# Transposed attention scores: the mask product is replaced by a tile that GpSimd writes, one slot later

## The reference

```python
q = proj(query, w_q, b_q); k = proj(key, w_k, b_k); v = proj(value, w_v, b_v)
scores = jnp.einsum('bhqd,bhkd->bhqk', q, k) / np.sqrt(D_K)
scores = jnp.where(mask, scores, -jnp.inf)      # mask: j <= i
attn = jax.nn.softmax(scores, axis=-1)
out = jnp.einsum('bhqk,bhkd->bhqd', attn, v)
...
x = x + jnp.tanh(g_xattn[0]) * _L0_xattn_ref(_layernorm(x, axis=-1), ctx_1024, ctx_1024, ...)
x = x + jnp.tanh(g_ffn[0]) * _L0_ffn_ref(_layernorm(x, axis=-1), ...)
```

## Time and profile before

| | us |
|---|---|
| median of 3 runs | 938.75 (936.92 to 939.47) |
| the profiled execution | 942.84 |
| its span | 940.9 |

### The profile page before, as it was taken

One profiled execution on the slowest core, in us unless ns is written; L12 is line 12 of the kernel. 1 busy time (PEld: TensorE's weight loads), 2 busy tenths in 40 slices (PEclk: granted clock), 3 DMA queues, 4 the chain that ended last, 5 costly groups with the idle time before them and its releaser, 6 DMA issues. The chain is left out here.

```text
span 940.9 us, 24425 instructions
## 1 busy us (share of the span) xinstructions
PE 846.5 (90%) x7600; PEld 750.5 (80%) x7601; DVE 600.4 (64%) x1521; ACT 442.3 (47%) x962; POOL 257.6 (27%) x239
## 2 busy tenths in 40 slices
PE   3599999999999999999539999999999999999990
PEld 2488888888888888888338789998989998989980
DVE  2357888888888888887636555555555555555540
ACT  2155555655555555654224444554444455544440
POOL 3001333222332333323210322232332232223332
PEclk9699999999999999999659999999999999999996
DMA  8765666665667787864388432323233233322222
GB/s 185 141 135 132 158 152 129 139 155 156 155 159 202 188 185 176 174 164 156 130 288 295 87 53 48 54 53 53 48 50 52 48 59 50 51 48 36 30 24 25
DMA packets 87944, 108.77 MB, mean 116 GB/s; under 512 B 12832, under 2 KB 81568, under 8 KB 85664
## 3 DMA queue, kind: packets, MB, share of 16 engines
q1 hardware_dynamic: 72448, 87.17, 37.4%
q0 software_dynamic: 14304, 19.15, 12.7%
q10 hardware_dynamic: 1088, 1.11, 0.4%
HBM read 46.82 MB, written 34.36 MB: 86 GB/s over the span
## 5 line engine op out<-in xcount | busy, mean ns | idle before, releaser
L1220 POOL DMA_INDIRECT out_rows<-yg,xs x78 | 126.6, 1624 | 332.7 <-ACT yg L1262 190.3
L1352 PE MATMUL bank<-xh,wts 128*128 128x256 f16 x1872 | 214.2, 275 | 0.0
L1368 PE MATMUL bank<-wts,hh 128*128 x1872 | 210.6, 273 | 0.0
L1352 PEld LDWEIGHTS bank<-xh,wts 128*128 x1872 | 185.0, 99 | 22.5
L1368 PEld LDWEIGHTS bank<-wts,hh 128*128 128x128 f16 x1872 | 183.2, 98 | 21.2
L1252 ACT ACTIVATE hf<-bank,b1t,gscale 128x256 f32<-128x256 f32 x312 | 154.7, 562 | 24.3 <-PE bank L1352 24.3
L979 PE MATMUL bank<-va,probs 128*128 128x102 f32 x1024 | 139.7, 278 | 8.1 <-DVE ao L696 8.1
L979 PEld LDWEIGHTS bank<-va,probs 128*128 128x128 f32 x1024 | 124.2, 192 | 10.7 <-DVE ao L696 6.2
L1262 ACT ACTIVATE yg<-yb,xs 128x256 f32<-128x256 f32 x78 | 35.4, 500 | 199.5 <-DVE yb L1301 199.5
L583 ACT ACTIVATE probs<-bank 128x512 f32<-128x512 f32 x128 | 76.9, 601 | 101.8 <-PE bank L962 95.2
L1291 DVE SCALAR_TENSOR_TENSOR hh<-hf,hscale,hh 128x512 f16<-128x512 f32 x156 | 117.1, 751 | 5.6
(11 more groups left out here) (169 smaller groups left out, 1082.0 us busy)
## 6 DMA issues: line engine op xcount, KB each, us to landing
wts<-in_W SPq DMA_DIRECT2D x16, 1024.0 KB, 7.9
wts<-keys SPq DMA_DIRECT2D x96, 128.0 KB
wts<-queries SPq DMA_DIRECT2D x96, 128.0 KB
xs<-token_rows SPq DMA_DIRECT2D x39, 272.0 KB
split_weights<-wts SPq DMA_DIRECT2D x8, 1024.0 KB, 4.6
wts<-split_weights SPq DMA_DIRECT2D x8, 1024.0 KB
xin<-in_x SPq DMA_DIRECT2D x16, 256.0 KB, 4.0
cin<-in_ctx_in SPq DMA_DIRECT2D x16, 256.0 KB, 4.2
```

What stands on the lines that cost most here:

```text
L1220: pool.indirect_dma_start(out=out[:, :], out_offset=bass.IndirectOffsetOnAxis(ap=numbers, axis=0), in_=yg[m % 2][:, half, :], in_offset=No ...
L1352: last = pe.matmul(HB[c // 2][:, c % 2 * TILE:(c % 2 + 1) * TILE], wts[:, bass.ds(expert[1], 1), at:at + P], xh[b][:, xp, k, :], start=q = ...
L1368: last = pe.matmul(YB[b][:, half * D:(half + 1) * D], hh[b][:, hp, c, half * P:(half + 1) * P], wts[:, bass.ds(expert[0], 1), at:at + D], ...
```

## The change

GpSimd now makes one tile `cover` per quad, 128 queries by 4 x 128 keys. Where the key is not after the query it holds the query's row maximum, elsewhere 1e30. It does this with one `affine_select`, from `rowmax` broadcast along the keys. Four products of this tile with the negative identity then bring both the maxima and the mask into the transposed scores, and the product of identity and mask is gone. The transposed scores of a quad run two slots behind its scores, not one, and the exponentials with them; the probabilities' products stay three slots behind. The row maxima's buffer is now freed by the select (`cover_ready`), the cover's by the transposed scores. `cover` lies in memory of the expert stage's first input tiles, which the attention stage doesn't use. GpSimd's indirect DMAs go from slots 4, 5, 6, 7 to 3, 4, 6, 7.

```diff
-MASKED = -1e30
+MASKED = 1e30
...
+        cover = [env["first_xs"][0][:, :, :].rearrange("p h r -> p (h r)")[:, 256 * i:256 * i + 256].bitcast(BF16)
+                 .rearrange("p (a k) -> p a k", a=4) for i in range(2)]
...
                 def it(g, par, half, stays, stayed):
                     for n in range(QUADS):
+                        if there(g):
+
+                            pool.wait_ge(max_ready, g * QUADS + n + 1)
+                            settled(pool)
+                            when(pool, n >= 2 or there(g - 1), st_psum, g * QUADS + n - 1)
+                            settled(pool)
+                            pool.affine_select(out=cover[n % 2][:, :, :],
+                                               in_=rowmax[n % 2][:, :].unsqueeze(2).to_broadcast([P, 4, P]),
+                                               compare_op=ALU.is_ge, fill=MASKED, base=0, pattern=[[0, 4], [-1, P]],
+                                               channel_multiplier=1).then_inc(cover_ready, 1)
                         if n in (1, 5) and there(g - 1):
                             b = n // 4
                             pool.wait_ge(var2_ready, (g - 1) * GT + b + 1)
...
-                        if n >= 4 and there(g - 2):
-                            b, r = (n - 4) // 2, n % 2
-                            if n == 4:
+                        if n in (3, 4, 6, 7) and there(g - 2):
+                            b, r = divmod((3, 4, 6, 7).index(n), 2)
+                            if n == 3:
...
-                        q, pg = (QUADS - 1, g - 1) if n == 0 else (n - 1, g)
+                        q, pg = (QUADS + n - 2, g - 1) if n < 2 else (n - 2, g)
...
-                            when(dve, n >= 2 or there(g - 1), st_psum, g * QUADS + n - 1)
+                            when(dve, n >= 2 or there(g - 1), cover_ready, g * QUADS + n - 1)
...
-                        if there(g if n >= 1 else g - 1):
-
-                            tg, m, i = (g, n - 1, par) if n >= 1 else (g - 1, QUADS - 1, p1)
+                        if there(g if n >= 2 else g - 1):
+
+                            tg, m, i = (g, n - 2, par) if n >= 2 else (g - 1, QUADS + n - 2, p1)
                             tok = slice((m // 4) * P, (m // 4) * P + P)
-                            pe.wait_ge(max_ready, tg * QUADS + m + 1)
+                            pe.wait_ge(cover_ready, tg * QUADS + m + 1)
                             when(pe, m >= 2 or there(tg - 1), exp_ready, tg * QUADS + m - 1)
                             ps = TB[m % 2]
-                            pe.matmul(ps[:, :], ident16[:, :], maskT[:, :].unsqueeze(1).to_broadcast([P, 4, P]),
-                                      start=True, stop=False)
-                            for a in range(4):
-                                pe.matmul(ps[:, a * P:(a + 1) * P], rowmax[m % 2][:, a:a + 1].to_broadcast([P, P]),
-                                          negident[:, :], start=False, stop=False)
                             for a in range(4):
                                 h = 4 * (m % 4) + a
+                                pe.matmul(ps[:, a * P:(a + 1) * P], cover[m % 2][:, a, :],
+                                          negident[:, :], start=True, stop=False)
                                 last = pe.matmul(ps[:, a * P:(a + 1) * P], kst[i][:, h, tok],
-                                                 qst[i][:, h, tok], start=False, stop=a == 3)
+                                                 qst[i][:, h, tok], start=False, stop=True)
```

## The result

| | median us (lowest to highest) |
|---|---|
| before | 939.04 (936.92 to 939.47) |
| after | 1022.34 (1020.48 to 1023.27) |

The ratio is 1.0889, with an interval from 1.0866 to 1.0913: the change costs 8.9%. The forecast was 961 with a range of 935 to 984. The direction was right, the size was not: +83 us in place of +22.

The account below looks back on a forecast made before the run. TensorE was taken to bound each group up to slot 4's residual, a VectorE chain from there to `ao`. Per group -0.86 + 1.56 + 0.3 = +1.0, together +14, clock +8: +22, so 961 us, range 935 to 984.

Parts of the forecast that it names:

- the queue and the chain: Slots 4 to 7: the power waits behind slot 5's select, `norm2` starts 1.56 us later, VectorE's work grows 5.88 to 7.44.
- the clock term: Attention groups: TensorE's pauses of 2.0 and 1.6 us lower its clock in half the groups or more, costing 8 us.
- it falls in every group: Rival, attention groups: the clock falls in every group, nearly all exposed, 25 us instead of 8, giving 978; chance 0.15.
- the first part: Slot 0 to slot 4's second output projection: TensorE drops five masks, 1.08 us, but VectorE's lateness leaves 0.86 saved.
- contention: Shared port: the select after row maximum 2 meets a two-input VectorE instruction, costing 0.3 us per group (0 to 0.9).
- so the lateness stays: Behind slot 1's select: `norm2` is 0.53 us later; VectorE, busy 7.32 of 7.79 us up to 310.46, stays late.
- the end of the stage: End of the attention stage: one slot more in the drain costs about 0.5 us.
- the 953 of the prediction: Sign of a wrong forecast: a granted clock of 1.00 throughout would put the result near 953.
- The port rival: Selects 0, 2, 3, 6, 7 block two-input VectorE instructions, up to 0.9 us each; 15 us more, 976; chance 0.15.
- `norm2` beside `xb`: Slot 5: `norm2` takes 1.36 us beside `xb`, cited as agreeing with two-input VectorE and GpSimd instructions excluding each other.
- The faster rival: Attention groups: the two-slot lag lifts TensorE's waits and powers are not held; 36 us gained, about 901; chance 0.12.
- a mask product taken from TensorE inside them gives nothing: From slot 4's residual to `ao`, 5.88 us: VectorE sets the pace, so dropping mask products there gains nothing.

Follow-up runs that it names:

- filled: The changed kernel plus unread products in TensorE's two pauses, 16 in slot 6 and 12 in slot 7: 969.4 us, ratio 1.0327.
- both powers first: The changed kernel with GpSimd's power for `rs2` moved ahead of the select in slots 1 and 5: 960.7 us, ratio 1.0231.
- both powers first and the pauses filled: The changed kernel with the powers ahead of the selects and 16 unread products in slot 7 alone: 936.2 us, ratio 0.9943.
- the change in its best form: The changed kernel with the powers ahead of the selects and `xb` at the very start of slot 0: 930.9 us, ratio 0.9903.
- the short chain: The kernel before with `xb` moved to the end of slot 7 and slot 6's weight split behind `ao`: 959.8 us, ratio 1.0211.
- the kernel without such a meeting of `xb` and `norm2`: The kernel before with `xb` moved from slot 5 to the start of slot 0: 927.7 us, ratio 0.9860.

## Why the prediction was wrong

**Right: the queue and the chain, the exact figure by luck.** The step that the power stands behind the select gave a chain from 5.88 to 7.44 and pauses of 2.0 and 1.6. Measured 7.44 (mean), 1.8 and 0.9 to 1.5. Two terms in it were off against each other: the select takes 0.64 and not 0.80, and what lies between the row maximum's end and the select's start is 0.34 as a rule (0.65 at 328.57), not 0.15, since the select's buffer is read until then. Both together put `norm2` 1.54 later, where the forecast had 1.56. I had seen that wait for select 1 and not for select 5. The select's duration, 150 to 450 us, ns min/median/max:

```profile
L496 POOL TENSOR_SCALAR_AFFINE_SELECT xs<-rowmax x75: 626/638/835, 152.3 to 446.7; 128x512 bf16<-128x512 bf16 x75
```

The Trainium skill ("GPSIMD Engine Reference", section "Performance versus the Vector engine") has 769 ns for 512 elements as a best case; this trace has less, 638, and the measurement decides.

**Wrong, and most of the miss: the size of the clock term.** The forecast took one stretch of 3.4 us at half pace, in half of the groups, two thirds of it exposed: 8 us. The runs show 53 (after less filled). It falls in every group, it lasts longer (8.9 us per group in the mean, 6.8 in the one shown), and most of it lies behind `ao`, where TensorE is the bound, so that 3.9 of the 4.5 us that it takes are exposed. The rival "it falls in every group", 25 us, had the first and third right but kept the length of the one stretch that the trace of before had. With 53 in place of 8, the forecast of 961 becomes 1006.

**Wrong: the first part.** The forecast was -0.86 for TensorE and +0.3 for contention. It counted five masks; one of them stands ahead of the keys' projection and so in the third cut, where it shows as 5.95 to 5.72 with the clock held. For keys to residual that leaves about -0.34 (-0.86 + 0.22 + 0.3). The change has +0.32 there. With both powers first it is 13.96 - 14.47 = -0.51, close to four masks less contention (-0.56), so these prices hold where select 1 is out of the way. The step that failed is the one on VectorE's lateness behind select 1, "so the lateness stays", from which "the residual can start at 313.36 - 0.93 + 0.04 = 312.47": I let the slack ahead of the residual absorb the lateness, and didn't see that TensorE itself waits for VectorE in slot 3, for `ao` of the second batch. The power in slot 1 costs 0.83 per group (14.79 against 13.96), 12 us in all. That is most of what is left between 1006 and 1022.

**Wrong: the end of the stage.** The forecast had "about +0.5" for one slot more in the drain. With the lag alone it is 1.1 from the last keys' projection to the experts (83.9 against 82.8), but 10.0 in the change and 8.0 with the pauses filled, of which the last group's own length explains 5.5 and 1.7. The change has a wait of TensorE for `ao` of 3.9 us there (510.7), where the kernel before has 1.5; what makes it so long stays open. This and the first part are why a clock of 1.00 gives 969.4 (filled), and not the 953 of the prediction.

**Contention: right, a size off.** The port rival had up to 1.0 per group. Of the tile `sel`, the instruction beside select 2, before and after:

```profile
L808 DVE TENSOR_TENSOR sel<-sel,pos x11: 281/284/288, 174.4 to 434.5; 128x128 f32<-128x128 f32 x11
```

```profile
L813 DVE TENSOR_TENSOR sel<-sel,pos x10: 718/720/722, 161.9 to 447.0; 128x128 f32<-128x128 f32 x10
```

That is 0.44 in each group, where I had 0.3. The select that meets such an instruction takes 0.83 in place of 0.64. The prediction gave `norm2` beside `xb` as a case of two inputs; `norm2` has one tile and two numbers per row as inputs, so it is none, though it is held up all the same. `sel` has two.

**The faster rival** counted on 36 us. In the kernel with both powers first and the pauses filled, pitch falls by 0.67 per group, 10 us. Of the rest of the 1.72, 0.44 go to contention, and three masks (0.65) lie in the VectorE chain, as the forecast had it: "a mask product taken from TensorE inside them gives nothing".

## What to carry to other kernels

When a change lets TensorE wait, price what follows the wait and not only the wait: here pauses of some 1.8 and 1.3 us come with 1.6 more in the chain and 3.9 in half-speed products behind it, and an experiment with unread products in the pauses separates the two. Before an instruction goes to a lightly loaded engine, look at what stands behind it on that engine's queue, and for whom. Where another engine sets the end of a stretch, removing TensorE's work from it gives nothing; taking the engine that blocks that chain out of it (`xb` to another slot, one block moved) gave at least as much as the change in its best form (0.9860 against 0.9903).

## What the runs showed of the hardware

- Pauses of 1.16 to 1.26 us were enough to bring TensorE to its lower level of 1.2 GHz for a while in five of twelve cases, in groups of which the rest ran dense; two pauses, of 1.7 to 2.0 and 0.9 to 1.5 us, brought it down in every group. The length of a pause alone doesn't decide: single pauses of 1.77 to 1.85 us brought it down in nine of eleven cases with the powers first, and in the kernel before with the short chain five of six pauses of 1.59 to 1.87 us left it at 1.00. Products whose result nobody reads held it at 1.00.
- A GpSimd select of 512 bf16 elements takes 0.64 us where one of 128 took 0.30.
- Beside `xb` (1.26 us on GpSimd) a VectorE `scalar_tensor_tensor` with two inputs in on-chip memory takes 1.76 us in place of 0.74, and `norm2` 1.35 in place of 0.41. In both meetings `xb` starts 0.05 us earlier and keeps its 1.26, so the exchange on GpSimd's queue only chose which VectorE instruction is held up.
- An indirect DMA on GpSimd takes 0.97 to 1.50 us also in the kernel without such a meeting of `xb` and `norm2` (row of tile `pay` above); what lengthens it wasn't looked into.
